# Where projections, transposed maxima and their low parts stand within a double step of a fused attention and feed-forward kernel

## What is computed

```python
x = x + layernorm(attention(layernorm(x)))     # 16 heads of 64, softmax over 2048 keys
x = x + layernorm(ffn(layernorm(x)))           # 128 -> 32 -> 512 -> gelu -> 32 -> 128
# attention: q, k, v = x Wq + bq, x Wk + bk, x Wv + bv;  softmax(q k^T / 8) v;  then Wo, bo
```

## Time and profile before

| what | value |
|---|---|
| time, median of 3 runs | 2533.64 us (2533.57 to 2534.62) |
| the profiled execution | 2539.57 us, of which the span is 2537.8 us |
| mean granted clock of TensorE | 0.981 |
| TensorE busy | 2433.8 us (96%) |
| VectorE busy | 2070.6 us (82%) |
| ScalarE busy | 2163.1 us (85%) |
| GpSimd busy | 2008.5 us (79%) |

### The profile page before, as it was taken

One profiled execution on the slowest core, in us unless ns is written; L12 is line 12 of the kernel. 1 busy time (PEld: TensorE's weight loads), 2 busy tenths in 40 slices (PEclk: granted clock), 3 DMA queues, 4 the chain that ended last, 5 costly groups with the idle time before them and its releaser, 6 DMA issues.

```text
span 2537.8 us, 44015 instructions
## 1 busy us (share of the span) xinstructions
PE 2433.8 (96%) x15728; PEld 1197.3 (47%) x15728; DVE 2070.6 (82%) x3171; ACT 2163.1 (85%) x2454; POOL 2008.5 (79%) x1095
## 2 busy tenths in 40 slices
PE   4999999999999999999999999999999999998885
PEld 2454454545445454544545454454445454454332
DVE  6788888888888888888888888888888888888877
ACT  2788889888988889888888988888888888887884
POOL 1588888888888888888888888888888888887673
PEclk7899999999999999999999999999999999999997
DMA  1010001000000000100010000000001001000011
GB/s 40 18 31 18 22 26 32 14 26 26 25 21 26 26 14 26 31 26 14 26 32 21 20 26 26 19 26 26 26 14 31 26 18 29 26 26 22 26 34 29
DMA packets 60771, 63.11 MB, mean 25 GB/s; under 512 B 25900, under 2 KB 44204, under 8 KB 60556
## 3 DMA queue, kind: packets, MB, share of 16 engines
q1 hardware_dynamic: 60556, 60.30, 7.9%
HBM read 57.40 MB, written 2.62 MB: 24 GB/s over the span
## 4 chain that ended last, share of the span: by engine, by line
PE 85%; DVE 13%; issue 1%; ACT 1%; DMA 0%; POOL 0%; POOLq 0%; ACTq 0%; DVEq 0%
PE o_ps L361 37%; PE spare_ps L314 15%; PE score_ps L342 8%; PE score_ps L345 7%; PE score_ps L348 7%; DVE max_part L672 5%; PE spare_ps L282 2%; PE spare_ps L291 2%; PE spare_ps L300 2%; PE spare_ps L391 2%; DVE q_lo L694 2%; DVE k_lo L688 2%; PE spare_ps L373 1%; DVE ln_stats L629 1%; DVE z_sb L640 1%
## 5 line engine op out<-in xcount | busy, mean ns | idle before, releaser
L870 POOL TENSOR_TENSOR total<-total,probs 128x832 f32<-128x832 f32 x896 | 1767.1, 1972 | 364.2 <-ACT probs L541 290.9
L672 DVE TENSOR_REDUCE max_part<-spare_ps 128x1 f32<-128x512 f32 x2020 | 1309.5, 686 | 321.8 <-PE spare_ps L314 307.2
L541 ACT ACTIVATE probs<-score_ps 128x1024 f32<-128x1024 f32 x1024 | 994.9, 1022 | 263.0 <-PE score_ps L348 252.0
L531 ACT ACTIVATE score_ps<-m_all 128x1024 f32<-128x1024 f32 x1024 | 1011.6, 1032 | 7.6 <-PE score_ps L328 6.2
L361 PE MATMUL o_ps<-probs,v_sb 128*64 128x512 f32 x4096 | 998.3, 609 | 0.0
L314 PE MATMUL spare_ps<-k_hi,q_hi 64*128 64x512 f32 x2020 | 477.2, 467 | 29.0 <-DVE max_part L672 12.2
L361 PEld LDWEIGHTS o_ps<-probs,v_sb 128*64 128x64 f32 x4096 | 250.0, 137 | 451.7 <-issue 323.6
L342 PE MATMUL score_ps<-q_hi,k_hi 64*128 64x512 f32 x2048 | 417.8, 403 | 6.0 <-ACT score_ps L531 5.9
L345 PE MATMUL score_ps<-q_lo,k_hi 64*128 64x512 f32 x2048 | 406.5, 392 | 0.0
L348 PE MATMUL score_ps<-q_hi,k_lo 64*128 64x512 f32 x2048 | 406.2, 391 | 0.0
L703 DVE TENSOR_REDUCE part_sum<-probs 128x192 f32<-128x768 f32 x256 | 393.4, 1537 | 5.0 <-ACT probs L541 5.0
(11 more groups left out here) (87 smaller groups left out, 1085.4 us busy)
## 6 DMA issues: line engine op xcount, KB each, us to landing
m_all<-m_scratch SPq DMA_DIRECT2D x64, 512.0 KB, 3.7
denom<-denom_scratch SPq DMA_DIRECT2D x126, 128.0 KB, 2.9
xg<-in_L_attn_x SPq DMA_DIRECT2D x14, 256.0 KB, 3.0
block_out<-z_sb SPq DMA_DIRECT2D x8, 256.0 KB, 2.3
m_scratch<-max_rows SPq DMA_DIRECT2D x64, 4.0 KB
denom_col<-denom SPq DMA_DIRECT2D x63, 4.0 KB
denom_scratch<-denom_col SPq DMA_DIRECT2D x63, 4.0 KB, 1.4
w_qkv<-in_L_attn_Wk SPq DMA_DIRECT2D x8, 64.0 KB, 2.9
```

The costliest lines, as they stand in the source:

```text
L531: nc.scalar.activation(score_ps[st % 2][:], m_all[:, G % 2], ACT.Copy).then_inc(s["seed_done"], 1)
L541: nc.scalar.activation(probs[:, st % RING], score_ps[st % 2][:], ACT.Exp, scale=SCALE).then_inc(s["exp_done"], 1)
L672: nc.vector.reduce_max(max_part[:, G % 2, h, qt, kc:kc + 1], bank[max_bank(n, h)], AX.X).then_inc(s["max_done"], 1)
L870: nc.gpsimd.tensor_tensor(others(total[:, G % 2]), so_far, others(probs[:, st % RING]), ALU.add).then_inc(s["sum_done"], 1)
```

## The change

It moves the added work of a double step and its read-outs. On TensorE, keys, values, queries, transposed maxima and the output projection come after the second maxima and before the values. On ScalarE, the high parts and the read-out of the transposed maxima come behind the seeds of the same double step. On VectorE, the low parts come first in the following double step, both first maxima behind them; the values' projection and the output projection are read after the second maxima. The double steps of keys, values and queries are others, and the ring is dealt out in the new order.

```diff
-K_AT = {(0, 0): 0, (0, 6): 1, (1, 0): 2, (1, 6): 3}
-V_AT = {(2, 0): 0, (2, 6): 1, (3, 0): 2, (3, 6): 3}
+K_AT = {(0, 6): 0, (1, 4): 1, (1, 6): 2, (2, 4): 3}
+V_AT = {(0, 7): 0, (1, 7): 1, (2, 7): 2, (3, 7): 3}
-Q_AT, M_AT = 4, 5
+Q_AT, M_AT = 3, 5
...
 (pe_program; spare_banks likewise)
+                me.ffn(n, 0)
+                if 2 * n + LEAD < STEPS:
+                    me.max_pair(2 * n + LEAD)
+                me.scores(2 * n)
+                me.scores(2 * n + 1)
+                if 2 * n + LEAD < STEPS:
+                    me.max_pair(2 * n + LEAD + 1)
                 if (c, d) in K_AT and u + 1 < UNITS:
                     me.project_k(u + 1, K_AT[c, d])
...
                 if projected_at(G, d) is not None:
                     me.out_projection(projected_at(G, d))
-                me.ffn(n, 0)
-                if 2 * n + LEAD < STEPS:
-                    me.max_pair(2 * n + LEAD)
-                me.scores(2 * n)
-                me.scores(2 * n + 1)
-                if 2 * n + LEAD < STEPS:
-                    me.max_pair(2 * n + LEAD + 1)
                 me.ffn(n, 1)
...
 (act_program)
+                act_ffn(act, n, 0)
+                act_exp(act, 2 * n)
+                act_exp(act, 2 * n + 1)
+                if n + 1 < DOUBLES:
+                    act_seed(act, 2 * n + 2)
+                    act_seed(act, 2 * n + 3)
                 if (c, d) in K_AT and u + 1 < UNITS:
                     act_k(act, u + 1, K_AT[c, d])
                 if d == Q_AT and G + 2 < CHUNKS:
                     act_q(act, G + 2)
                 if d == M_AT and G + 1 < CHUNKS:
                     act_m(act, G + 1)
-                act_ffn(act, n, 0)
-                act_exp(act, 2 * n)
-                act_exp(act, 2 * n + 1)
-                if n + 1 < DOUBLES:
-                    act_seed(act, 2 * n + 2)
-                    act_seed(act, 2 * n + 3)
...
 (dve_program)
+            def low_parts(n):
+                G, u, c, d = n // PER_CHUNK, n // (PER_CHUNK * NC), n // PER_CHUNK % NC, n % PER_CHUNK
+                if n >= 0 and (c, d) in K_AT and u + 1 < UNITS:
+                    dve_k(dve, u + 1, K_AT[c, d])
+                if n >= 0 and d == Q_AT and G + 2 < CHUNKS:
+                    dve_q(dve, G + 2)
...
-                if (c, d) in V_AT and u + 1 < UNITS:
-                    dve_v(dve, u + 1, V_AT[c, d])
+                low_parts(n - 1)
                 dve_low(dve, n)
-                if projected_at(G, d) is not None:
-                    dve_y(dve, projected_at(G, d))
                 more = 2 * n + LEAD < STEPS
                 if more:
                     dve_max(dve, 2 * n + LEAD, 0)
-                if (c, d) in K_AT and u + 1 < UNITS:
-                    dve_k(dve, u + 1, K_AT[c, d])
-                if d == Q_AT and G + 2 < CHUNKS:
-                    dve_q(dve, G + 2)
-                if more:
                     dve_max(dve, 2 * n + LEAD, 1)
...
                 if more:
                     dve_max(dve, 2 * n + LEAD + 1, 0)
                     dve_max(dve, 2 * n + LEAD + 1, 1)
+                if (c, d) in V_AT and u + 1 < UNITS:
+                    dve_v(dve, u + 1, V_AT[c, d])
+                if projected_at(G, d) is not None:
+                    dve_y(dve, projected_at(G, d))
                 if d == NEG_MAX_AT and G + 1 < CHUNKS:
                     dve_neg_max(dve, G + 1)
```

More of the change, by code:

```diff
@@ L87, in spare_banks @@
         G, u, c, d = n // PER_CHUNK, n // (PER_CHUNK * NC), n // PER_CHUNK % NC, n % PER_CHUNK
+        for stage, g in ffn_pe(n, 0):
+            use(stage, g)
         if n < DOUBLES:
+            for st in (2 * n + LEAD, 2 * n + LEAD + 1):
+                for h in range(2 if st < STEPS else 0):
+                    use("max", 2 * st + h)
             if (c, d) in K_AT and u + 1 < UNITS:
@@ L98, in spare_banks @@
                 use("Wo", projected_at(G, d))
[L99 to L104, removed]
         if n == END_L:
```

## The result

| what | before | changed |
|---|---|---|
| time, median of 4 runs | 2534.13 us | 2579.04 us |
| the profiled execution, span | 2537.8 us | 2581.3 us |

The ratio is 1.0178 (95% interval 1.016 to 1.0195): slower by 44.9 us. The forecast was 2571.6, 7 us too low and inside its range (2551 to 2590).

A forecast was written before the change was run, and what follows sets the result against it. TensorE's queue was taken to set the time. Losses of 7.12 us a unit against 4.66 before, over 15 units plus about 1 us, gave +38 on 2533.64: 2571.6 us, range 2551 to 2590.

The forecast's parts named there:

- VectorE, the low parts: Low parts queued ahead of both first maxima delay TensorE's second maxima: 0.69 us, six times, 4.14 a unit.
- The release: On TensorE, second maxima start 0.06 us after their bank's release, so 2.31 us after the first maxima.
- The projections behind late maxima: On TensorE, projections in double steps with delayed second maxima wait 0.17 us for their bank, four times: 0.68 a unit.
- six late uses: TensorE's late bank uses in a unit; missed waits could cost up to 0.10 us more each, estimated 9 us in all.
- The keys' low parts at (1,5) and (2,5): On VectorE, these two low parts fall behind a part sum and a longer double step, costing about nothing.
- At (0,5) and (3,5): Late part sums on VectorE delay TensorE's second maxima and transposed maxima: 0.40 us together, twice, 0.80 a unit.
- The sum: Losses in a unit go from 4.66 to 7.12 us, +2.46; 15 units give 36.9, the last about +1.
- Seeds and transfers: Waiting for ScalarE's seeds costs 6 x 0.25 us, 1.50 a unit as before; SyncE's later transfer of maxima costs nothing.
- the waits for low parts: Sign in the profile after: these waits disappear from TensorE's list, while its waits for maxima go up.
- Rival 2: ScalarE's high parts are ready early, so bank waits go and none comes: -3.2 us a unit, about 2486; chance 6%.

The follow-up runs named there:

- Run 2: Kernel before, with only VectorE's low parts of keys and queries moved ahead of the first of the first maxima: 2586.13 us, ratio 1.0195.
- runs 3 and 4: Changed kernel, with ScalarE's high parts of keys and queries between the two seeds (2504.13 us) or ahead of both seeds (2513.59 us), respectively.
- run 5: Changed kernel, with TensorE's projections of keys and queries and transposed maxima behind the values of their double step: 2591.05 us, ratio 1.0219.

## Why the prediction was right, and what it missed

**The main step held.** "VectorE, the low parts" had q_hi ending at A+0.86 (0.87), q_lo from 0.90 (0.91), the first reading to 2.25 (2.26). Run 2 isolates it, runs 3 and 4 remove it from the other side.

**The release was mis-sized.** I took 0.06 from a release to the second maxima, from a place where a low part releases them; B then stands at 2.31. It stands at 2.41: the reading ends at 1034.18 and the matmul starts at 1034.33, 0.15 later. So 0.79 and not 0.69. The kernel before had this price already, behind a reading in its own (1,5):

```profile
1020.88 0.39 PE L348 MATMUL score_ps<-q_hi,k_lo 64*128 64x512 f32 x2
1021.11 0.49 PE L314 MATMUL spare_ps<-k_hi,q_hi 64*128 64x512 f32 x2
```

The reading that starts at 1020.27 ends at 1020.95, 0.15 ahead of 1021.11. Where a projection follows, the extra 0.10 is absorbed, since that waits for the later reading anyway; it is left at (0,4) and (3,4), 0.2 a unit.

**The projections behind late maxima held.** (1,4) and (1,7) last 5.64, as the sum has it (2.41 is later, the projection at 2.91 isn't). The Trainium skill's page "TensorE: Matmul & The Clock Gate" ("Step-by-step: what each phase is for") says that weight loads are pulled ahead of running matmuls. The extra 0.10 for each of six late uses, which I had put beside it as an upper end, didn't come.

**The keys' low parts at (1,5) and (2,5) were mis-sized.** I had them at "about nothing". B isn't late there (1039.28, A+1.72), but k_lo stands ahead of both readings, the later reading ends at 1039.66, and the transposed maxima, which need its bank, start at 1039.71, 0.43 behind B and not 0.33. (1,5) lasts 4.23, not 3.92+0.24 = 4.16; twice a unit this makes 0.16. At (0,5) and (3,5), TensorE after, the sum came out with one term wrong:

```profile
998.69 0.50 PE L313 MATMUL spare_ps<-k_hi,q_hi 64*128 64x512 f32 x2
...
1000.65 0.50 PE L313 MATMUL spare_ps<-k_hi,q_hi 64*128 64x512 f32 x2
1001.15 0.32 PE L320 MATMUL spare_ps<-ident,neg_max 128*64 128x128 f32 x1
```

B stands at A+1.96 and not 1.86, but the transposed maxima wait for the later reading and start at A+2.46, where I had 2.45. The double step lasts 4.54; my terms give 4.56.

**The sum.** My terms give 149.54 for a unit, and it takes 149.99. Of the 0.45 between them the release makes 0.2, the keys' low parts 0.16, and d = 1 0.17 (5.08 in each chunk, where 3.92+0.25+0.87 is 5.04); small differences take 0.1 off. From (0,0) of the first unit to that of the last, 15 units took 2205.9 us before and 2250.8 after, +44.9, against my 36.9. 14 of them have 2.9 each. The first has 4.1; why it loses more isn't settled. What comes after them is 0.5 longer, what comes before 1.9 shorter.

**Seeds and transfers.** As forecast, d = 1 waits for its seeds in every chunk, and the later transfer of the maxima costs next to nothing: the waits of seeds for it are 3.0 us in all, the longest 1.0, and were 1.3 us before.

**One sign was wrong.** I had the waits for low parts gone from TensorE's list. The one for q_lo is still there, 56.5 us, and was 30.4 before. It is an idle time of the weight loads: in (1,4) 0.92 of it are put down to q_lo, and the matmul's own 0.52 behind it to the reading, which ended last.

**Rival 2**, the other side, was the mechanism that runs 3 and 4 then built: q_hi had to end before A+0.25 of the next double step. Between the seeds it ends 0.06 before that double step begins, and 1.25% is what comes of it; the rival's 2486 isn't reached (2504.13). The forecast was right that the change itself doesn't get there: behind the seeds is where q_hi stood all along.

## What to carry to other kernels

When a producer is moved earlier, follow it through every queue to the consumer. Here TensorE's projection came 2 us earlier, but ScalarE's slot for it didn't, and VectorE's slot was moved ahead of work that was on the critical path; together with the new spread these moves made a loss of 45 us, and one line moved on ScalarE turned it into a gain of 30. An instruction that waits should stand behind the ready work that others need, or its input should be moved first.

## What the runs showed of the hardware

From a bank's release to TensorE's next matmul it took one of two times. It was 0.05 to 0.06 us for second maxima behind a low part (1016.79 to 1016.85 in the kernel before) and for a projection behind a reading (1034.77 to 1034.83 after). It was 0.15 for second maxima behind a reading (1034.18 to 1034.33). How long TensorE had stood idle doesn't decide it: the 0.15 is there after 0.52 (1034.33), after 0.05 (1000.65, behind a reading that ends at 1000.50) and with scores still running (1021.11), and the 0.06 behind q_lo came after an idle of 0.07.

What goes with it in nearly all places is which of the pair's two banks came last, the first one (a low part's, 0.05) or the second (a reading's, 0.15); run 5 has 0.10 at (2,5). No run isolates it, so the cause stays open.

After a late B the values follow 0.43 behind it (1016.85 to 1017.28) and not 0.33 (1003.19 to 1003.52).
